# Layer 0's first attention: who subtracts the maxima of the local tiles, in how many pieces the exponential runs, and by how many rows the scores are made

## The chip, the cores and the metric

The kernel runs on one core of a Trainium2 chip. The metric is device microseconds (us) of one execution. Three executions of the kernel before took 1293.5 to 1294.74 us, with a median of 1294.52 us.

## The reference, cut to what matters

A decoder of four layers over `x` (8 batches of 128 tokens, 128 features). Each layer adds three blocks to `x`: an attention, a cross attention (or what takes its place) and a mixture of experts. The change touches only the attention of layer 0. It has 16 heads of 8 features, and each head combines three branches with a softmaxed gate: attention over compressed blocks of 16 keys, attention over the keys of the blocks chosen by rank, and attention over a local window:

```python
x = x + _L0_attn_ref(_layernorm(x, axis=-1), L0_attn_Wq, L0_attn_Wk, L0_attn_Wv, L0_attn_Wo, L0_attn_Wck, L0_attn_Wcv, L0_attn_Wg, L0_attn_bg)
```

For a head, both the chosen and the local branch start from the same scores `q @ k.T`, add their own mask (causal plus choice, or window), take the softmax over the keys of each query, and multiply by the values. A softmax does not change when the maximum is subtracted first; the kernel does so to keep the exponential in range, and divides by the sum after the values, which carry a column of ones.

## The kernel before, in words

One program holds five instruction streams (PE, VectorE, ScalarE, GpSimd and the DMA queue) that meet in semaphores. Each engine runs its stream in the order written.

The part that matters here is the loop of `layer0_attention_pe`, `_act`, `_pool` and `_dve` over 32 steps, with 9 more to drain it. Step k stands for batch k // 4 and the heads 4 * (k % 4) to 4 * (k % 4) + 3: four heads, 128 queries, 128 keys, one tile of 128x512. The work of step k:

- GpSimd multiplies the keys of the batch by a mask of four columns (`mask_keys`, L471; its line in the trace is L474), so that in each of four copies only the 8 rows of one head are left: one 128x512 tile `kM` a step. It is written up to four steps ahead, into four buffers; VectorE makes the first.
- PE multiplies all 128 rows of the queries with it (`score_pe`, L514), into banks 0 and 1 in turn.
- VectorE adds the causal mask (L874) and the window mask (L876) to the scores and so makes two tiles, chosen and local. It then takes the local tile's four maxima (`lower_dve`, L551) and multiplies them by minus the scale (L553, 128x4).
- GpSimd adds the choice of blocks to the chosen tile (L757), before the masking of keys for step k + 4.
- One step later VectorE takes the chosen tile's maxima and scales them (L551, L553 again).
- ScalarE computes `exp(scale * s + bias)` in place. The bias is a column, one for each head, so that a tile takes four instructions of 128x128 (`exp_heads_act`, L545). In a step it first copies turned tiles out of PSUM (L530), then runs the chosen tile of k - 1, then the local tile of k.
- Three steps later PE transposes both tiles (L523), ScalarE copies them out (L530), and five steps later PE multiplies the values (L534), four heads side by side.
- Once in four steps a batch is complete. ScalarE copies two banks of results (L726), PE turns them back (L540), and VectorE unpacks them in `unpack`: a reciprocal (L835), a product of 128x16 of two SBUF tiles (L837), a product with the bank (L842), and in the second unpack two sums (L858, L860). Then come a transpose (L562), its copy (L573), the output product (L567) and the sum into `x` (L578).

With k % 4 written as a residue: VectorE's unpack of the chosen heads falls ahead of the masks of a step with residue 1, the second unpack with its sums ahead of residue 2, and the sum into `x` ahead of residue 0. In PE's stream the output product opens a step of residue 0, and the scores of a step are its last work. ScalarE's copy of the results (L726) falls at residue 0, and the small copy for the output (L573) at residue 3.

The layer's cross attention (`batches_*`, from L909) already does it the other way: four copies of the keys are masked once a batch with `mask4` (L903), each of its score products takes 32 rows (L922), GpSimd subtracts the maxima (L1065), and a single exponential covers a tile (L981).

Of the kernel before, what the change touches and what calls it, by code (L numbers as in the profile page):

```python
# [11 lines left out]
ALU = mybir.AluOpType  # L12
ACT = mybir.ActivationFunctionType
AX = mybir.AxisListType

P = 128
# [104 lines left out]
def build_program(nc, d, out):  # L121
    with ExitStack() as ctx:
# [321 lines left out]
        def heads_memory(tiles, probs, outputs):  # L444
            used_ = dict(kM=[carve(4, P) for _ in range(4)], o=[carve(P) for _ in range(2)],
# [7 lines left out]
        def heads_signals(tiles, lowered=True):  # L453

            n = 4 * NB
            s = dict(km_dve=signal("km_dve", 1), km_pool=signal("km_pool", n - 1), vp=signal("vp", NB),
# [5 lines left out]
            if lowered:  # L462
                s["lowered"] = signal("lowered", n)
# [3 lines left out]

        def km_ready(eng, s, k):
            eng.wait_ge(*(s["km_pool"](k) if k else s["km_dve"](1)))

        def mask_keys(eng, kM, kT, k):  # L471

            b, g = divmod(k, 4)
            return eng.tensor_tensor(kM, kT[:, b * P:(b + 1) * P].unsqueeze(1).broadcast_to([P, 4, P]),  # L474
                                     bc(mask16[:, 4 * g:4 * g + 4], 2, P), ALU.mult)
# [14 lines left out]
        def stage_keys_pool(pool, s, m, kT, k):  # L490
            if k >= 4:
                pool.wait_ge(*s["scored"](k - 3))
            mask_keys(pool, m["kM"][k % 4], kT, k).then_inc(s["km_pool"].sem, 1)

        def stage_keys_values_pool(pool, s, m, kT, v, vp, k_out, v_out):

            pool.wait_ge(*pool_step.now())
            for k in range(2):
                pool.wait_ge(*k_out(k))
            for k in range(4 * NB):  # L500
                if k:
                    stage_keys_pool(pool, s, m, kT, k)
                if k == 1:
                    for i in range(2):
                        pool.wait_ge(*v_out(i))
                if k % 4 == 1:
                    stage_values_pool(pool, s, k // 4, v, vp, 1)

        def score_pe(pe, s, m, k, qT):
            b = k // 4  # L510
            km_ready(pe, s, k)
            if k >= 2:
                pe.wait_ge(*s["masked"](k - 1))
            pe.matmul(banks[k % 2][:, :], qT[:, b * P:(b + 1) * P], m["kM"][k % 4].rearrange("p j t -> p (j t)"),  # L514
                      start=True, stop=True).then_inc(s["scored"].sem, 1)

# [178 lines left out]
        def layer0_attention_act(act):  # L695
# [19 lines left out]
            for step in range(32 + 9):  # L715
# [21 lines left out]
                if k < 32:  # L737
# [2803 lines left out]
```

## Time and profile before

| what | value |
|---|---|
| median of three executions | 1294.52 us |
| the profiled execution: its own time | 1286.18 us |
| its span, first to last instruction | 1284.2 us |
| outside the span | 2.0 us |
| mean granted TensorE clock, share of full speed | 0.896 |
| VectorE busy in the span | 771.8 us (60%) |
| ScalarE busy | 656.8 us (51%) |
| GpSimd busy | 337.2 us (26%) |
| the loop, first to last window mask | 72.48 to 198.82 us |

How to read it: the trace times each instruction on its engine, from the span's start. A busy share over the whole span is a mean over many stages, so that what bounds this loop has to be read in its own 126 us. A timeline row gives start, duration, engine, line, operation and count, and in brackets the idle time ahead of it with the instruction that ended it. Consecutive instructions of one engine that don't depend on one another overlap by some 0.08 us.

### The profile page before, as it was taken

The numbers are of one execution on the slowest core, as the hardware profiler recorded it, in microseconds if no ns is written. First come the engines' busy times: TensorE is split into PE (matmuls) and PEld (weight loads), VectorE is DVE, ScalarE is ACT, GpSimd is POOL, SyncE is SP. The second block draws the span as 40 slices with busy tenths as digits, with TensorE's granted clock in tenths as the row PEclk, the third lists the DMA queues.
The fourth block names the chain that finished last, engine by engine and source line by source line (L and its number), as shares of the span: only waits on it lengthen the run. The fifth ranks groups of instructions, "written<-read, shape, count | busy, mean of one in ns | idle before, by whom it ended". The sixth has DMA issues, their size and how long they took to land. (4 is left out here: it accounts for less than half of the span.)

```text
span 1284.2 us, 22278 instructions
## 1 busy us (share of the span) xinstructions
PE 1010.8 (79%) x8221; PEld 758.4 (59%) x8221; DVE 771.8 (60%) x1870; ACT 656.8 (51%) x1688; POOL 337.2 (26%) x440
## 2 busy tenths in 40 slices
PE   6257877783779767779999989997789961878998
PEld 4224444352776355579976765775358850546898
DVE  4889995783323766752246665665777667764422
ACT  1168885561445646736538774775113223763433
POOL 2254542662222134410003331333410031111000
PEclk9689897896889778999999999999689995998999
DMA  7200000002555000020000000000120000000000
GB/s 246 85 1 1 2 1 18 1 1 66 150 166 198 1 1 2 2 99 1 1 2 1 2 2 1 2 2 33 79 107 26 1 1 0 2 1 1 1 1 17
DMA packets 31978, 42.46 MB, mean 33 GB/s; under 512 B 7592, under 2 KB 25632, under 8 KB 30592
## 3 DMA queue, kind: packets, MB, share of 16 engines
q1 hardware_dynamic: 30848, 38.95, 9.1%
q0 software_dynamic: 1024, 2.10, 0.5%
q8 instruction: 66, 1.08, 0.4%
q14 instruction: 40, 0.33, 0.1%
HBM read 35.54 MB, written 5.51 MB: 32 GB/s over the span
## 5 line engine op out<-in xcount | busy, mean ns | idle before, releaser
L1287 ACT ACTIVATE arena<-bank,w_L_ffn_b1T 128x512 f32<-128x512 f32 x128 | 86.9, 688 | 98.5 <-PE bank L1229 98.0
L1264 PEld LDWEIGHTS bank<-bufB,arena 128*128 128x128 f32 x1024 | 118.9, 192 | 2.4
L1264 PE MATMUL bank<-bufB,arena 128*128 128x128 f32 x1024 | 119.6, 275 | 0.0
L2525 ACT ACTIVATE arena<-arena 128x128 f32<-128x128 f32 x256 | 99.2, 390 | 20.0 <-DVE arena L2552 20.0
L293 POOL TENSOR_TENSOR norm_rstd<-norm_std,minus_half 128x4 f32<-128x4 f32 x24 | 25.4, 1060 | 316.0 <-DVE norm_std L288 316.0
L2536 POOL TENSOR_TENSOR arena<-arena 128x512 f32<-128x512 f32 x64 | 66.5, 1040 | 151.8 <-DVE arena L2585 151.8
L1324 DVE SCALAR_TENSOR_TENSOR x<-bank,gate_c,x 128x128 f32<-128x128 f32 x128 | 36.0, 344 | 114.9 <-PE bank L1264 114.7
L545 ACT ACTIVATE arena<-arena 128x128 f32<-128x128 f32 x256 | 80.3, 395 | 42.3 <-DVE arena L553 42.3
L1229 PE MATMUL bank<-x_high,w_low 128*128 128x512 f32 x200 | 85.7, 429 | 8.1 <-DVE w_low L1238 5.5
L1229 PE MATMUL bank<-x_high,w_high 128*128 128x512 f32 x200 | 81.1, 405 | 0.0
L1229 PE MATMUL bank<-x_low,w_high 128*128 128x512 f32 x200 | 81.0, 405 | 0.0
L2548 DVE SCALAR_TENSOR_TENSOR arena<-bank,bufA 128x512 f32<-128x512 f32 x64 | 43.8, 685 | 35.2 <-PE bank L2474 35.2
L2848 ACT ACTIVATE arena<-bank 128x512 f32<-128x512 f32 x36 | 21.6, 599 | 61.2 <-PE bank L1229 61.2
L514 PE MATMUL bank<-arena 128*128 128x512 f32 x64 | 37.3, 674 | 18.9 <-DVE arena L474 18.9
L2396 PE MATMUL bank<-xnT,bufA 128*128 128x512 f32 x96 | 50.7, 627 | 1.6 <-ACT arena L341 1.6
L341 ACT ACTIVATE arena<-bank 128x512 f32<-128x512 f32 x36 | 21.5, 596 | 58.7 <-PE bank L2396 39.3
L757 POOL TENSOR_TENSOR arena<-arena 128x512 f32<-128x512 f32 x32 | 33.8, 1057 | 64.4 <-DVE arena L876 64.4
L2445 PE MATMUL bank<-arena 128*64 128x128 f32 x512 | 42.1, 285 | 10.7 <-ACT arena L2516 10.5
L1229 PEld LDWEIGHTS bank<-x_high,w_low 128*128 128x128 f32 x200 | 39.4, 197 | 17.1 <-DVE w_low L1238 6.0
L2431 PEld LDWEIGHTS bank<-arena 128*128 128x128 f32 x256 | 36.7, 191 | 21.2 <-issue 14.1
L963 ACT ACTIVATE arena<-bank 128x512 f32<-128x512 f32 x64 | 36.7, 598 | 23.5 <-PE bank L939 23.1
L2525 ACT ACTIVATION_READ_ACCUMULATOR arena<-arena 128x1 f32 x256 | 48.3, 189 | 0.0
(489 smaller groups left out, 2555.6 us busy)
## 6 DMA issues: line engine op xcount, KB each, us to landing
bufB<-in_L_ffn_w SPq DMA_DIRECT2D x28, 256.0 KB
bufA<-in_L_ffn_w SPq DMA_DIRECT2D x2, 2048.0 KB, 9.8
bufB<-in_L_ffn_W SPq DMA_DIRECT2D x2, 2048.0 KB
bufB<-in_L_ffn_w SPq DMA_DIRECT2D x2, 2048.0 KB
bufA<-in_L_ffn_Wgu SPq DMA_DIRECT2D x1, 2304.0 KB, 9.0
bufA<-in_L_attn_Wqkv SPq DMA_DIRECT2D x1, 2048.0 KB, 8.8
rows<-blank SPq DMA_DIRECT2D x2, 960.0 KB, 6.9
results<-arena SPq DMA_DIRECT2D x6, 256.0 KB
```

What stands on the lines that cost most here:

```text
L514: pe.matmul(banks[k % 2][:, :], qT[:, b * P:(b + 1) * P], m["kM"][k % 4].rearrange("p j t -> p (j t)"), start=True, stop=True).then_inc(s[ ...
L545: m = act.activation(tile[:, j * P:(j + 1) * P], tile[:, j * P:(j + 1) * P], ACT.Exp, bias=low[:, j:j + 1], scale=SCALE)
L963: act.activation(m["p"][n % 4], banks[4 + n % 2][:, :], ACT.Copy).then_inc(s["probs"].sem, 1)
L1229: m = pe.matmul(bank[:, :], a[:, ws], b[:, c], start=n == 0, stop=n == 2)
L1264: i = pe.matmul(bank[:, j * P:(j + 1) * P], h[:, f, j * P:(j + 1) * P], w2[:, u * FF + f * P:u * FF + (f + 1) * P], start=f == 0, stop=f = ...
L1287: act.activation(m["h"][k % 2][:, f, :], banks[f][:, :], ACT.Gelu, bias=b1[:, c:c + 1]).then_inc(g["hidden"].sem, 1)
L2396: o = pe.matmul(bank[:, :], w[:, c * P:(c + 1) * P], xnT[:, i * BANK:(i + 1) * BANK], start=True, stop=True)
L2431: o = pe.matmul(banks[7][:, u * P:(u + 1) * P], b2["oT"][k % 2][:, j * P:(j + 1) * P], b2_wo[:, c:c + P], start=False, stop=k == UNITS - 1 ...
L2445: o = pe.matmul(banks[5 + k % 2][64 * t:64 * t + 64, j * P:(j + 1) * P], b2["v"][gg % 2][:, 4 * u + 2 * j + r, :], b2["p"][(U0 + k) % 3][: ...
L2525: o = act.activation(tile, tile, ACT.Exp, bias=b2["mn"][n % 8][:, j:j + 1], scale=-1.0, accum_out=b2["sm"][n % 8][:, j:j + 1])
L2536: pool.tensor_tensor(tile, tile, bc(b2["rs"][n % 4], 2, P), ALU.mult).then_inc(g["over_sum"].sem, 1)
L2548: dve.scalar_tensor_tensor(tile, banks[r][:, :], -1.0 / np.sqrt(DH).item(), bias[:, h0:h0 + 4, :].rearrange("p h t -> p (h t)"), ALU.mult, ...
```

## The change

Four things, in one loop:

- VectorE no longer scales the local tile's maxima; it only takes them and signals `peak`.
- GpSimd waits for `peak` and subtracts the maxima from the local tile in place (128x512), right after it has added the choice to the chosen tile.
- ScalarE computes the local tile's exponential in one instruction of 128x512, with no bias. The chosen tile keeps its four.
- The keys are masked once a batch instead of once a step: one tile `kM` of four copies, in each of which one head out of every four consecutive ones is left, in two buffers. PE's score product takes the 32 rows that hold the four heads of the step. GpSimd masks the next batch after the first subtraction of a batch. Its first use still comes from VectorE.

```diff
--- before.py
+++ after.py
@@ -442,7 +442,7 @@
 
 
         def heads_memory(tiles, probs, outputs):
-            used_ = dict(kM=[carve(4, P) for _ in range(4)], o=[carve(P) for _ in range(2)],
+            used_ = dict(kM=[carve(4, P) for _ in range(2)], o=[carve(P) for _ in range(2)],
                          oT=[carve(P) for _ in range(2)], rs=[carve(H) for _ in range(2)],
                          res=[carve(BANK) for _ in range(2)], a=[carve(BANK) for _ in range(tiles)],
                          p=[carve(BANK) for _ in range(probs)], mx=[carve(4) for _ in range(2 * 8)])
@@ -453,26 +453,17 @@
         def heads_signals(tiles, lowered=True):
 
             n = 4 * NB
-            s = dict(km_dve=signal("km_dve", 1), km_pool=signal("km_pool", n - 1), vp=signal("vp", NB),
+            s = dict(km_dve=signal("km_dve", 1), km_pool=signal("km_pool", NB - 1), vp=signal("vp", NB),
                      scored=signal("scored", n), masked=signal("masked", n), exped=signal("exped", n),
                      turned=signal("probs_turned", tiles * n), probs=signal("probs", tiles * n),
                      valued=signal("valued", tiles * n), res=signal("res", tiles * NB),
                      back=signal("heads_back", tiles * NB), weighed=signal("weighed", tiles * NB),
                      oturned=signal("o_turned", NB), oT=signal("oT", NB), projected=signal("projected", NB))
             if lowered:
-                s["lowered"] = signal("lowered", n)
+                s["peak"], s["lowered"] = signal("peak", n), signal("lowered", n)
             if tiles == 2:
                 s["chosen"], s["lowered2"], s["exped2"] = (signal(i, n) for i in ("chosen", "lowered2", "exped2"))
             return s
-
-        def km_ready(eng, s, k):
-            eng.wait_ge(*(s["km_pool"](k) if k else s["km_dve"](1)))
-
-        def mask_keys(eng, kM, kT, k):
-
-            b, g = divmod(k, 4)
-            return eng.tensor_tensor(kM, kT[:, b * P:(b + 1) * P].unsqueeze(1).broadcast_to([P, 4, P]),
-                                     bc(mask16[:, 4 * g:4 * g + 4], 2, P), ALU.mult)
 
         def pad_values_pool(pool, vp):
             for t in vp:
@@ -487,32 +478,19 @@
             pool.tensor_copy(vp[b % 4][:, :, 0:HD],
                              v[:, b * P:(b + 1) * P].rearrange("p (h c) -> p h c", c=HD)).then_inc(s["vp"].sem, 1)
 
-        def stage_keys_pool(pool, s, m, kT, k):
-            if k >= 4:
-                pool.wait_ge(*s["scored"](k - 3))
-            mask_keys(pool, m["kM"][k % 4], kT, k).then_inc(s["km_pool"].sem, 1)
-
-        def stage_keys_values_pool(pool, s, m, kT, v, vp, k_out, v_out):
-
-            pool.wait_ge(*pool_step.now())
-            for k in range(2):
-                pool.wait_ge(*k_out(k))
-            for k in range(4 * NB):
-                if k:
-                    stage_keys_pool(pool, s, m, kT, k)
-                if k == 1:
-                    for i in range(2):
-                        pool.wait_ge(*v_out(i))
-                if k % 4 == 1:
-                    stage_values_pool(pool, s, k // 4, v, vp, 1)
-
         def score_pe(pe, s, m, k, qT):
-            b = k // 4
-            km_ready(pe, s, k)
+            b, g = divmod(k, 4)
+            rows = slice(32 * g, 32 * g + 32)
+            pe.wait_ge(*(s["km_pool"](b) if b else s["km_dve"](1)))
             if k >= 2:
                 pe.wait_ge(*s["masked"](k - 1))
-            pe.matmul(banks[k % 2][:, :], qT[:, b * P:(b + 1) * P], m["kM"][k % 4].rearrange("p j t -> p (j t)"),
+            pe.matmul(banks[k % 2][:, :], qT[rows, b * P:(b + 1) * P], m["kM"][b % 2][rows, :, :].rearrange("p j t -> p (j t)"),
                       start=True, stop=True).then_inc(s["scored"].sem, 1)
+
+        def mask_batch_keys(eng, kM, kT, u):
+
+            return eng.tensor_tensor(kM, kT[:, u * P:(u + 1) * P].unsqueeze(1).broadcast_to([P, 4, P]),
+                                     bc(mask4[:, :], 2, P), ALU.mult)
 
         def turn_pe(pe, s, n, tile, exped):
 
@@ -735,8 +713,9 @@
                     exp_heads_act(act, h["a"][(2 * k) % 8], h["mx"][8 + k % 8], s["exped2"])
                 k = step
                 if k < 32:
+                    tile = h["a"][(2 * k + 1) % 8]
                     act.wait_ge(*s["lowered"](k + 1))
-                    exp_heads_act(act, h["a"][(2 * k + 1) % 8], h["mx"][k % 8], s["exped"])
+                    act.activation(tile, tile, ACT.Exp, scale=SCALE).then_inc(s["exped"].sem, 1)
 
         def layer0_attention_pool(pool):
             t, g, m, s, h = a0, a0g, a0m, a0s, a0h
@@ -747,17 +726,21 @@
             pool.wait_ge(*m.out(6))
             pool.wait_ge(*m.out(7))
             pool.wait_ge(*m.out(2))
+            pool.wait_ge(*m.out(3))
             stage_values_pool(pool, s, 0, t["v"], t["vp"], 2)
-            for k in (1, 2, 3):
-                stage_keys_pool(pool, s, h, t["kT"], k)
             for k in range(32):
                 b, gr = divmod(k, 4)
                 tile = h["a"][(2 * k) % 8].rearrange("p (r c) -> p r c", c=G0)
                 pool.wait_ge(*s["masked"](k + 1))
                 pool.tensor_tensor(tile, tile, bc(t["sel"][:, b * H + 4 * gr:b * H + 4 * gr + 4, :].rearrange(
                     "p h n -> p (h n)"), 2, G0), ALU.add).then_inc(s["chosen"].sem, 1)
-                if k + 4 < 32:
-                    stage_keys_pool(pool, s, h, t["kT"], k + 4)
+                local = h["a"][(2 * k + 1) % 8].rearrange("p (j t) -> p j t", t=P)
+                pool.wait_ge(*s["peak"](k + 1))
+                pool.tensor_tensor(local, local, bc(h["mx"][k % 8], 2, P), ALU.subtract).then_inc(s["lowered"].sem, 1)
+                if gr == 0 and b + 1 < NB:
+                    if b:
+                        pool.wait_ge(*s["scored"](4 * b))
+                    mask_batch_keys(pool, h["kM"][(b + 1) % 2], t["kT"], b + 1).then_inc(s["km_pool"].sem, 1)
                 if gr == 0 and b + 1 < NB:
                     stage_values_pool(pool, s, b + 1, t["v"], t["vp"], 2)
 
@@ -825,7 +808,7 @@
             dve.wait_ge(*dve_step.now())
             dve.tensor_scalar(t["sel"], t["sel"], 1.0, BIG, ALU.subtract, ALU.mult).then_inc(g["selected"].sem, 1)
             dve.wait_ge(*m.out(2))
-            mask_keys(dve, h["kM"][0], t["kT"], 0).then_inc(s["km_dve"].sem, 1)
+            mask_batch_keys(dve, h["kM"][0], t["kT"], 0).then_inc(s["km_dve"].sem, 1)
 
             def unpack(n, u):
 
@@ -876,7 +859,8 @@
                     dve.tensor_tensor(h["a"][(2 * k + 1) % 8].rearrange("p (j t) -> p j t", t=P), s3,
                                       bc(window[:, :], 1, 4), ALU.add).then_inc(s["masked"].sem, 1)
                     dve.wait_ge(*s["masked"](k + 1))
-                    lower_dve(dve, h["a"][(2 * k + 1) % 8], h["mx"][k % 8], s["lowered"])
+                    dve.tensor_reduce(h["mx"][k % 8], h["a"][(2 * k + 1) % 8].rearrange("p (j t) -> p j t", t=P), AX.X,
+                                      ALU.max).then_inc(s["peak"].sem, 1)
 
 
 
@@ -897,11 +881,6 @@
             else:
                 s.update(peak=signal("peak", NB), lowered=signal("lowered", 3 * NB))
             return s
-
-        def mask_batch_keys(eng, kM, kT, u):
-
-            return eng.tensor_tensor(kM, kT[:, u * P:(u + 1) * P].unsqueeze(1).broadcast_to([P, 4, P]),
-                                     bc(mask4[:, :], 2, P), ALU.mult)
 
 
         def nothing(*_):
```

## Rows read from the trace of the kernel before

**Rows 1.** Page, part 1: busy time by engine, after the span.
```profile
span 1284.2 us, 22278 instructions
```
**Rows 2.** Stretches: length, then busy time by engine, granted clock, DMA share, GB/s.
```profile
166.00:182.00 16.00, 11.75 (x115) 7.37 (x115) 15.25 (x32) 14.06 (x42) 7.97 (x9) 1.00 0.01 2
...
114.00:118.00 4.00, 4.00 (x22) 2.48 (x14) 2.28 (x6) 4.00 (x13) 1.93 (x2) 0.57 0.00 0
```
**Rows 3.** Waits in 70 to 210 us: who for whom, us in total, times, longest.
```profile
DVE arena L874 <- PE bank L514: 7.3, 8, 2.2
```
**Rows 4.** Timeline, window mask of steps 23 to 27, 30 and 31.
```profile
166.44 0.67 DVE L876 TENSOR_TENSOR arena<-bank,window 128x512 f32<-128x512 f32 x1
...
170.04 0.68 DVE L876 TENSOR_TENSOR arena<-bank,window 128x512 f32<-128x512 f32 x1
...
174.53 0.68 DVE L876 TENSOR_TENSOR arena<-bank,window 128x512 f32<-128x512 f32 x1
...
179.67 0.68 DVE L876 TENSOR_TENSOR arena<-bank,window 128x512 f32<-128x512 f32 x1
...
183.02 0.68 DVE L876 TENSOR_TENSOR arena<-bank,window 128x512 f32<-128x512 f32 x1
...
195.56 0.68 DVE L876 TENSOR_TENSOR arena<-bank,window 128x512 f32<-128x512 f32 x1
...
198.82 0.68 DVE L876 TENSOR_TENSOR arena<-bank,window 128x512 f32<-128x512 f32 x1
```
**Rows 5.** Timeline, step 26 to step 27, a step without an unpack.
```profile
180.43 1.05 POOL L757 TENSOR_TENSOR arena<-arena 128x512 f32<-128x512 f32 x1 [3.08 <-DVE arena L876]
181.10 0.40 DVE L553 TENSOR_SCALAR arena<-arena 128x4 f32<-128x4 f32 x1
181.44 1.04 POOL L474 TENSOR_TENSOR arena<-arena,mask 128x512 f32<-128x512 f32 x1
181.51 0.69 DVE L551 TENSOR_REDUCE arena<-arena 128x4 f32<-128x512 f32 x1
181.54 1.28 ACT L545 ACTIVATE arena<-arena 128x128 f32<-128x128 f32 x4 [1.08 <-DVE arena L553]
182.24 0.27 DVE L553 TENSOR_SCALAR arena<-arena 128x4 f32<-128x4 f32 x1
```
**Rows 6.** Timeline, from step 26's exponentials to the scores of step 28.
```profile
182.72 0.25 ACT L573 ACTIVATE arena<-bank 128x128 f32<-128x128 f32 x1
...
183.03 0.49 PE L567 MATMUL bank<-w_L_attn_Wo,arena 128*128 128x128 f32 x2 [1.83 <-ACT arena L573]
...
184.96 1.02 PE L514 MATMUL bank<-arena 128*128 128x512 f32 x2
...
186.02 0.69 DVE L874 TENSOR_TENSOR arena<-bank,causal 128x512 f32<-128x512 f32 x1 [0.17 <-PE bank L514]
```
**Rows 7.** Timeline, step 23's exponentials (with step 22's), and the wait of step 29.
```profile
167.26 2.44 ACT L545 ACTIVATE arena<-arena 128x128 f32<-128x128 f32 x8
...
190.45 0.69 DVE L874 TENSOR_TENSOR arena<-bank,causal 128x512 f32<-128x512 f32 x1 [0.48 <-PE bank L514]
```
**Rows 8.** Timeline, the small product of the unpack, beside a GpSimd instruction and alone.
```profile
176.56 0.81 DVE L837 TENSOR_TENSOR arena<-arena 128x16 f32<-128x16 f32 x1
...
188.66 0.18 DVE L837 TENSOR_TENSOR arena<-arena 128x16 f32<-128x16 f32 x1
```
**Rows 9.** Groups by line, 0 to 300 us: count, busy us, mean ns, idle before.
```profile
L1065 POOL TENSOR_TENSOR arena<-arena,bufB 128x512 f32<-128x512 f32 x32 | 33.2, 1040 | 17.9 <-DVE bufB L1039 17.5
...
L981 ACT ACTIVATE arena<-arena 128x512 f32<-128x512 f32 x32 | 20.1, 629 | 18.4 <-POOL arena L1065 18.4
...
L858 DVE TENSOR_TENSOR arena<-arena 128x128 f32<-128x128 f32 x8 | 2.3, 292 | 0.3
```
**Rows 10.** Timeline, four score products of the cross attention, 32 rows each.
```profile
242.51 1.14 PE L922 MATMUL bank<-bufB 32*128 32x512 f32 x8
```
**Rows 11.** Timeline, the two longest waits for scores inside the loop, steps 12 and 16.
```profile
117.61 0.69 DVE L874 TENSOR_TENSOR arena<-bank,causal 128x512 f32<-128x512 f32 x1 [1.65 <-PE bank L514]
...
136.06 0.69 DVE L874 TENSOR_TENSOR arena<-bank,causal 128x512 f32<-128x512 f32 x1 [1.67 <-PE bank L514]
```

## The prediction

> **What bounds it now.** The profiled execution took 1286.18 us, 2.0 more than its span [rows 1], and is 8.3 us below the median of the runs shown, 1294.52. I work a difference out in the profiled one and put it on the median. I take 0.2%, 2.6 us, as what a measurement of this kernel can tell from no change.
>
> The first view is the stretches. In 166 to 182 us VectorE is busy for 15.25 of 16 us, ScalarE for 14.06, PE for 11.75, GpSimd for 7.97, at the full clock [rows 2]. So VectorE looks like the bound, and ScalarE is near. The waits say that PE isn't far either: VectorE waits for its scores in eight steps, 7.3 us in all [rows 3].
>
> The timeline gives the rhythm. I write t for the start of a step's window mask (L876). The period at the full clock is 3.60, 4.49, 5.14 and 3.35 us: 16.58 from step 23 to 27 [rows 4]. I call a step by its k % 4.
>
> A plain step shows what VectorE is busy with [rows 5]. GpSimd adds the choice from t + 0.76 to t + 1.81. VectorE's scaling of four columns starts at t + 1.43, and takes 0.40 us: it ends 0.02 us after GpSimd's instruction. The second scaling takes 0.27 and ends 0.03 after the masking of keys. The product L837 is clearer: 0.81 us beside a masking of keys, 0.18 without one [rows 8]. So part of VectorE's "busy" is waiting for GpSimd to let go. The maxima of the chosen tile start at 181.51, 0.03 after GpSimd's 181.48: they wait for the chosen tile, not for the scaling.
>
> **The parts of the change.**
>
> *The scaling that goes.* 32 instructions of 0.40, some 13 us of VectorE's busy time. In a plain step nothing of it comes back: the next instruction waits for GpSimd's addition until t + 1.84 anyway [rows 5], and the other scaling stays held until t + 2.84, now by the subtraction in the masking's place. Residues 3 to 0 and 2 to 3 keep their length on VectorE's side. In a step with an unpack the reciprocal can start at t + 1.32 instead of t + 1.76. L837 then asks for the port at t + 1.60, during the addition, gets it as the scaling did, and ends at t + 1.84 instead of t + 2.84: 1.0 us earlier.
>
> *The subtraction on GpSimd.* 32 of 1.04 us [rows 9], for the 31 maskings of 1.04 that shrink to 7. GpSimd goes from 8.0 to about 9 of 16 us: not a bound. But the subtraction holds the port from t + 1.77 to t + 2.81. Of the second unpack, L842 reads a bank and passes; L858 (two SBUF tiles as L837, 0.29 alone) follows at t + 2.19, is held, and ends near 2.96 rather than 2.48 [rows 9]. So the interval of residue 1 to 2 gets 1.0 - 0.48, say 0.54, shorter: 4.60 for 5.14. No row shows L858 beside a GpSimd instruction; its ends are no hold (1.0 gained) and a full hold (0.5), and I take the hold, since L837 has the same form. The Trainium skill (SBUF — State Buffer, "Who interferes with whom") says the same of forms: two SBUF inputs contend with a GpSimd instruction that reads SBUF, a reduction or an instruction with one SBUF input doesn't, and the loser is blocked for the whole instruction. By it the gain is 0.5 and not 1.0.
>
> In the first unpack L842 is followed by the maxima and the kept scaling, which asks at t + 2.79, when the subtraction ends and the batch's masking (1.04) follows. If it loses the port it ends at t + 3.86; if it wins, at t + 2.98. I take the loss, an interval of 4.38; the win would be 3.5. At the full clock this decides nothing (below); in the two periods whose residue 0 comes late by a low clock [rows 11] the scores are ready by then, and a win is worth 0.8 each.
>
> *The signal to ScalarE comes later.* `lowered` was ready at t + 1.84, and will be at t + 2.85, after the addition and the subtraction. The exponential then takes 0.63 us instead of 1.28 [rows 5, 9]. It ends at t + 3.51, not t + 3.15: **0.36 later**. What waits for it is PE. In rows 6, step 26's exponential lets the small copy start at 182.72, the output product, values, transposes and scores of step 28 follow in PE's order, and the scores end at 185.98; VectorE, free at 185.85, waits 0.17. So from t(26) to t(28) the chain takes 6.96 us and sets the time. With 0.36 more it is 7.32, and the interval of residue 3 to 0 grows from 3.60 to 3.97.
>
> The same holds for the next one. Step 23's exponentials end at 169.70 = t + 3.26 [rows 7]; the copy of the results, the turn back, the values, transposes and scores of step 25 follow, and its mask starts at t(23) + 7.48. With the exponential ending at 3.51 that is 0.25 more, against 0.05 of slack: t(25) comes at t(23) + 8.29, not 8.09. That these scores are near the bound is shown in step 29: there L837 takes 0.18, and VectorE waits 0.48 for PE instead [rows 7, 8]. VectorE's own side, 3.97 + 4.38 = 8.35, is about the same. The 1.0 us gained in the first unpack is hence lost to the scores.
>
> *ScalarE.* 96 fewer instructions: 2.56 us of exponentials a step become 1.9. It is relieved, but it waits at every exponential, so that only the 0.65 counted above matters.
>
> *PE.* A product of 32 rows, two passes. Four of them took 1.14 us together [rows 10], one of 128 rows 1.02 [rows 6]. Apart from the first two, the new ones stand alone between transposes. I take 1.02 as before; the ends are 0.28 (the share of four) and 1.14. At the low end each score would come 0.74 us sooner, which would undo the 0.36 and give back up to 0.4 more a score-bound interval (some ten of them, -7 us with the 0.36s): I give it little, since each of the four is one of eight passes issued back to back.
>
> *Keys once a batch.* Each masking is ready three steps ahead, so the scores never wait. At the start the second score no longer waits for GpSimd's, but the first addition began at step 0's mask both ways: nothing. The added wait for the second half of the keys was over before the loop. No DMA is moved.
>
> **The sum.** A full-clock period: +0.26 for residues 3 to 1, -0.54, 0: -0.3. Five such periods have a masking of keys beside the unpack; where the period starts without the output product (once) or after a late step (once) the gain is 0.2: about -1.2 in all. The interval from step 3 to 4, at PE's pace, +0.36. The last period had no masking of keys to hold VectorE. Step 28's window mask is at 186.63, 0.61 after row 186.02 [rows 6]. From there to step 30 it took 8.93 and will take 4.32 + 4.60, and to step 31 it goes from 3.26 to 3.35 [rows 4]; with the 0.36 in front, +0.4. The drain starts from an exponential 0.2 later: +0.2. Total: -0.2 us, or -2 with the port won at residue 1. **Forecast: no change; in the profiled execution 1286.0 us, on the median 1294.3.**
>
> **The rivals.**
>
> *A, 50%: the sum holds*, from -2.5 to +2: 1292 to 1296.5.
>
> *B, faster, 27%.* The waits for scores are longest where the clock is low: 0.57 in 114 to 118 us [rows 2]; there VectorE waits 1.65 us for its scores, and 1.67 in step 16 [rows 11], each time 1.5 us more than the 0.17 of step 28. If a shorter second unpack, which shortens PE's pause in it, keeps the clock up, 3 us come back; if L858 isn't held, 0.5 in five periods; if the port is won, 1.6. Two of them, the first among them, give -4.6 to -5.5: about 1289.5. Against: the pauses that precede the low stretches are those of the output product.
>
> *C, slower, 23%.* That pause grows: PE has nothing from the end of step 27's scores to the output product, 1.83 us before [rows 6] and some 2.3 after. A long wait followed it in two of six periods. If it follows in all, four more at 1.5 are +6 us: 1300. It decides from two more on (+2.8). A lesser form of it: L837 just misses the port, which brings back 0.54 in five periods, +2.4.
>
> That the exponential of 128x512 isn't quicker than four is excluded by rows 9, where it takes 0.63.
>
> The range, 1289.5 to 1299, reaches to B and most of the way to C's 1300; what it leaves out is C in full and short scores. Chances: faster 0.27, same 0.50, slower 0.23.
>
> **What would show it.** The exponential's row 0.63 us, starting near t + 2.88. The chosen maxima in plain steps still at t + 1.84. L837 near 0.25 us; L858 near 0.75 in the second unpack; residue 1 to 2 at 4.6. VectorE's wait for scores (7.3 us) above 10, GpSimd's subtraction 1.04. The loop from 72.5 to some 198.5. Wrong would be: scores on time at residue 0, L837 still 0.8, or a change of the low-clock stretches.

## The result, and the profile of the changed kernel

The changed kernel takes 1304.0 us in the median of 13 runs, against 1294.5 for the kernel before: a ratio of 1.0088, with an interval from 1.0067 to 1.0110. It is slower by some 11 us. The forecast was no change, 1294.3 us, and its range ended at 1299.

The two profiled executions differ by more, 1302.2 against 1284.2 us of span, because the one of before was a short one (1286.18 us, where the median is 1294.5). The last sum into `x` of this attention starts at 227.0 us and not at 217.8. That is 9.2 us, about the difference of the medians (9.5), and the part that the change can explain. I look no further for the rest. The two rows, before and changed:

```profile
217.83 0.29 DVE L578 TENSOR_TENSOR x<-x,bank 128x128 f32<-128x128 f32 x1 [1.73 <-PE bank L567]
```

```profile
226.96 0.29 DVE L556 TENSOR_TENSOR x<-x,bank 128x128 f32<-128x128 f32 x1 [1.73 <-PE bank L545]
```

Page, part 1, of the changed kernel:

```profile
span 1302.2 us, 22159 instructions
```

The stretch 72 to 212 us, which holds the loop in both, first of the kernel before, then of the changed one (length; busy time of PE, PE's loads, VectorE, ScalarE, GpSimd; granted clock):

```profile
72.00:212.00 140.00, 102.63 (x908) 63.08 (x906) 121.94 (x255) 117.67 (x343) 64.24 (x68) 0.91 0.00 1
```

```profile
72.00:212.00 140.00, 115.64 (x809) 66.30 (x808) 109.14 (x213) 90.38 (x231) 73.82 (x78) 0.78 0.00 1
```

VectorE and ScalarE have less to do, as meant: 109 and 90 us of 140 instead of 122 and 118. Part of that is only that the changed kernel gets less far in the stretch; over the whole execution, where both kernels do the same work, VectorE is busy for 763.0 us instead of 771.8 and ScalarE for 636.7 instead of 656.8. PE is busy for longer, though the stretch ends before the changed kernel's drain, and its granted clock fell from 0.91 to 0.78. The waits of the changed kernel between 70 and 215 us say where that goes:

```profile
DVE arena L857 <- PE bank L487: 21.1, 13, 2.7
```

VectorE waited for scores for 7.3 us in eight steps [rows 3]; now it is 21.1 us in thirteen. L857 is the causal mask (L874 before), and L487 the score product (L514 before).

Summed over the loop's 31 intervals between window masks, by the residue of the step (step number modulo 4):

| from residue to residue | before, us | changed, us |
|---|---|---|
| 0 to 1 | 33.7 | 36.6 |
| 1 to 2 | 37.3 | 34.3 |
| 2 to 3 | 27.1 | 28.3 |
| 3 to 0 | 28.2 | 37.8 |
| all | 126.3 | 137.1 |

The loop is 10.8 us longer and the drain behind it 1.9 us shorter. Two of the 10.8 us are lost at once: the intervals from step 3 to 5, ahead of any output product, take 9.56 us for 7.47. In both kernels the clock is low when the loop starts; the kernel before has the full clock from some 73.5 us on (but for 83.7 to 87.1), the changed one only from some 91 us on. The stretch 76 to 82 us, before and changed:

```profile
76.00:82.00 6.00, 1.87 (x10) 0.81 (x8) 5.77 (x12) 4.20 (x15) 4.11 (x4) 1.00 0.00 0
```

```profile
76.00:82.00 6.00, 4.23 (x10) 1.93 (x10) 4.98 (x9) 3.20 (x10) 4.65 (x6) 0.50 0.00 0
```

One period of the changed kernel, from its timeline. L859 is the window mask (L876 before), L735 and L739 are GpSimd's addition and subtraction, L529 and L531 VectorE's maxima and scaling of the chosen tile, L718 the single exponential, L545 the output product and L501 the transposes:

```profile
113.49 1.10 PE L501 MATMUL bank<-ident,arena 128*128 128x128 f32 x8
...
114.52 1.12 PE L487 MATMUL bank<-arena 32*128 32x512 f32 x2
...
114.68 1.06 POOL L735 TENSOR_TENSOR arena<-arena 128x512 f32<-128x512 f32 x1 [2.55 <-DVE arena L859]
115.70 1.04 POOL L739 TENSOR_TENSOR arena<-arena 128x512 f32<-128x512 f32 x1
115.77 0.69 DVE L529 TENSOR_REDUCE arena<-arena 128x4 f32<-128x512 f32 x1 [0.45 <-POOL arena L735]
116.49 0.27 DVE L531 TENSOR_SCALAR arena<-arena 128x4 f32<-128x4 f32 x1
...
116.77 0.63 ACT L718 ACTIVATE arena<-arena 128x512 f32<-128x512 f32 x1 [1.85 <-POOL arena L739]
117.28 0.68 DVE L859 TENSOR_TENSOR arena<-bank,window 128x512 f32<-128x512 f32 x1
...
117.62 0.49 PE L545 MATMUL bank<-w_L_attn_Wo,arena 128*128 128x128 f32 x2 [1.98 <-ACT arena L551]
...
118.94 1.97 PE L501 MATMUL bank<-ident,arena 128*128 128x128 f32 x8
...
120.84 1.49 PE L487 MATMUL bank<-arena 32*128 32x512 f32 x2
...
122.37 0.69 DVE L857 TENSOR_TENSOR arena<-bank,causal 128x512 f32<-128x512 f32 x1 [2.25 <-PE bank L487]
...
122.97 0.68 DVE L859 TENSOR_TENSOR arena<-bank,window 128x512 f32<-128x512 f32 x1
```

With t = 113.92 for the window mask of that step, the chosen maxima start at t + 1.85, and the exponential at t + 2.85 for 0.63 us. These answer to 1.84 and 1.28 us in [rows 5], and to the prediction's t + 1.84 and t + 2.88. Then the transposes, which take 1.10 us at the full clock, take 1.97, and the interval is 5.69 us instead of 3.60 [rows 4]. PE's clock in those microseconds, from the view by stretches:

```profile
117.00:118.00 1.00, 0.38 (x2) 0.30 (x2) 0.97 (x3) 1.00 (x4) 0.00 (x0) 1.00 0.00 0
118.00:119.00 1.00, 1.00 (x18) 0.58 (x17) 0.87 (x2) 1.00 (x4) 0.97 (x1) 0.60 0.00 0
119.00:120.00 1.00, 1.00 (x6) 1.00 (x6) 0.84 (x2) 0.70 (x3) 1.00 (x2) 0.50 0.00 0
...
121.00:122.00 1.00, 1.00 (x2) 0.34 (x2) 0.00 (x0) 1.00 (x3) 0.00 (x0) 0.69 0.00 0
```

From some 118.2 to 121.6 us the clock is at the lower of its two levels (0.50, that is 1.2 GHz for 2.4). Five intervals from residue 3 to 0 hold an output product (the sixth product falls into the drain). In the kernel before two of them ran low, at 5.10 us; here all five do. In three of the five the clock falls at the output product, as above. In the other two, the steps 16 and 24, it had fallen some 4 us earlier, behind a pause of 1.41 us ahead of the transpose L540 (L562 before):

```profile
130.67 0.33 PE L540 MATMUL bank<-ident,arena 128*128 128x128 f32 x1 [1.41 <-DVE arena L843]
...
132.00:133.00 1.00, 1.00 (x6) 0.78 (x4) 0.96 (x3) 0.94 (x4) 0.31 (x1) 0.50 0.00 0
...
135.63 0.80 PE L545 MATMUL bank<-w_L_attn_Wo,arena 128*128 128x128 f32 x2 [0.45 <-ACT arena L551]
```

Where the clock is full, the changed kernel's intervals are 3.36, 4.36 and 4.60 us, no longer than the prediction had them. But for some 0.2 us in one step (3.57 us), what the loop loses it loses where the clock is low.

Three of VectorE's lines in the changed kernel (min, median and max in ns): the small product of the unpack (L837 before), the first sum of the second unpack (L858 before) and the kept scaling (L553 before):

```profile
L820 DVE TENSOR_TENSOR arena<-arena x16: 174/248/704, 104.8 to 224.1; 128x16 f32<-128x16 f32 x16
...
L841 DVE TENSOR_TENSOR arena<-arena x8: 291/754/757, 111.5 to 224.6; 128x128 f32<-128x128 f32 x8
...
L531 DVE TENSOR_SCALAR arena<-arena x32: 169/268/1039, 75.3 to 212.4; 128x4 f32<-128x4 f32 x32
```

### The profile page after: what moved, and what is told of

Read it like the earlier page. It is cut to its first block and busy times, and to the rows that moved or that the text cites. A ratio compares the mean times of both kernels' runs of the same rounds, so it can differ in the third digit from the quotient of the medians.

```text
span 1302.2 us, 22159 instructions
## 1 busy us (share of the span) xinstructions
PE 1037.1 (80%) x8221; PEld 774.8 (59%) x8221; DVE 763.0 (59%) x1838; ACT 636.7 (49%) x1592; POOL 345.5 (27%) x448
## 5 line engine op out<-in xcount | busy, mean ns | idle before, releaser
L2504 ACT ACTIVATE arena<-arena 128x128 f32<-128x128 f32 x256 | 99.2, 390 | 19.9 <-DVE arena L2531 19.9
L487 PE MATMUL bank<-arena 32*128 32x512 f32 x64 | 43.7, 800 | 20.4 <-DVE arena L492 18.9
L718 ACT ACTIVATE arena<-arena 128x512 f32<-128x512 f32 x32 | 20.2, 630 | 72.7 <-POOL arena L739 72.7
L501 PE MATMUL bank<-ident,arena 128*128 128x128 f32 x256 | 47.3, 343 | 6.9 <-ACT arena L508 6.1
L735 POOL TENSOR_TENSOR arena<-arena 128x512 f32<-128x512 f32 x32 | 33.9, 1058 | 68.0 <-DVE arena L859 68.0
L2424 PE MATMUL bank<-arena 128*64 128x128 f32 x512 | 42.1, 285 | 10.8 <-ACT arena L2495 10.5
```

The lines of the kernel that those rows point to most:

```text
L487: pe.matmul(banks[k % 2][:, :], qT[rows, b * P:(b + 1) * P], m["kM"][b % 2][rows, :, :].rearrange("p j t -> p (j t)"), start=True, stop=Tr ...
L501: t = pe.transpose(banks[2 + n % 2][:, j * P:(j + 1) * P], tile[:, j * P:(j + 1) * P], ident[:, :])
L2424: o = pe.matmul(banks[5 + k % 2][64 * t:64 * t + 64, j * P:(j + 1) * P], b2["v"][gg % 2][:, 4 * u + 2 * j + r, :], b2["p"][(U0 + k) % 3][: ...
L2504: o = act.activation(tile, tile, ACT.Exp, bias=b2["mn"][n % 8][:, j:j + 1], scale=-1.0, accum_out=b2["sm"][n % 8][:, j:j + 1])
```

## Two theories and the first four experiments

Two things in the change could do it. Theory **P**, my rival C: the later exponential makes PE's pause ahead of the output product longer, and the clock falls after it. Theory **R**: score products that use 32 of PE's 128 rows cost clock, and they are slower in themselves. I had not thought of R. Each half of the change was tried alone, R's edit alone, and all but R's edit. In this section the kernel before had a median of 1278.9 us on the chip used, and every ratio is to it.

**Scores by 32 rows, alone.** The kernel before, with one edit. The rows left out of the masked keys are zeros, so the result is the same:

```diff
-            pe.matmul(banks[k % 2][:, :], qT[:, b * P:(b + 1) * P], m["kM"][k % 4].rearrange("p j t -> p (j t)"),
+            rows = slice(32 * (k % 4), 32 * (k % 4) + 32)
+            pe.matmul(banks[k % 2][:, :], qT[rows, b * P:(b + 1) * P], m["kM"][k % 4][rows, :, :].rearrange("p j t -> p (j t)"),
```

> The kernel before, with one edit: the score product takes the 32 rows that are not zero instead of all 128; masking of keys, lowering and exponentials stay. Theory R (rows): the low clock comes with the products of 32 rows, and each also takes 0.2 us longer; then this alone is 5 to 10 us slower than before, the attention ends at 222 to 227 us instead of 217.8, and the clock falls after the output product in every period. Theory P (pause): the clock falls because PE's pause ahead of the output product ends later and is longer when the exponential comes 0.36 us later; then this stays within 0 to 3 us of before and the clock stays as before.

Measured: 1296.2 us, a ratio of 1.0128 (1.0083 to 1.0173). The attention ends at 236.7 us instead of 217.8. Its stretch 72 to 212 us, and rows of its timeline (L515 is its score product, L568 the output product, L524 the transposes, L875 and L877 the masks):

```profile
72.00:212.00 140.00, 121.21 (x760) 68.69 (x759) 112.38 (x229) 103.72 (x305) 63.62 (x68) 0.71 0.00 1
```

```profile
141.47 0.49 PE L568 MATMUL bank<-w_L_attn_Wo,arena 128*128 128x128 f32 x2
...
146.35 0.66 PE L541 MATMUL bank<-ident,arena 128*128 128x128 f32 x4 [1.74 <-ACT arena L727]
...
147.80 1.97 PE L524 MATMUL bank<-ident,arena 128*128 128x128 f32 x8
149.69 2.07 PE L515 MATMUL bank<-arena 32*128 32x512 f32 x2
151.81 0.69 DVE L875 TENSOR_TENSOR arena<-bank,causal 128x512 f32<-128x512 f32 x1 [2.31 <-PE bank L515]
152.41 0.68 DVE L877 TENSOR_TENSOR arena<-bank,window 128x512 f32<-128x512 f32 x1
...
155.65 2.07 PE L515 MATMUL bank<-arena 32*128 32x512 f32 x2
...
158.37 0.68 DVE L877 TENSOR_TENSOR arena<-bank,window 128x512 f32<-128x512 f32 x1
```

The clock is 0.71, lower than in the changed kernel, with lowering, exponentials and maskings as before. And the low stretch does not sit where P puts it: the output product at 141.47 follows the scores with no pause ahead of it (its row has no bracket), and the clock is down six microseconds later, over two whole steps (147.8 to 158 us; an interval of 5.96). A pause does come just before that fall, but another one: 1.74 us ahead of the turn back (L541), which the kernel before has too, up to 1.76 us long, with no fall behind it inside the loop. R is borne out, with 17 us where I gave it 5 to 10. The clock of the whole execution says so in every run: 0.870 to 0.875 in all six, 0.891 to 0.903 in 28 of the 29 of the kernel before (0.860 in one). My expectation had placed the fall after every output product; that part was wrong, since here the scores are so late that the output product no longer waits.

**The keys' part alone**, 32 rows included: the changed kernel with VectorE's scaling and ScalarE's four pieces put back.

```diff
-                pool.wait_ge(*s["peak"](k + 1))
-                pool.tensor_tensor(local, local, bc(h["mx"][k % 8], 2, P), ALU.subtract).then_inc(s["lowered"].sem, 1)
...
-                    act.activation(tile, tile, ACT.Exp, scale=SCALE).then_inc(s["exped"].sem, 1)
+                    exp_heads_act(act, h["a"][(2 * k + 1) % 8], h["mx"][k % 8], s["exped"])
```

> The changed kernel with VectorE scaling the local maxima and ScalarE in four pieces again, so that only the keys once a batch and the scores by 32 rows are left of the change. Theory R: 3 to 8 us slower than before (GpSimd's missing maskings give back up to 0.6 us a period). Theory P: no slower, likely 2 to 4 us faster, since the unpack is no longer held by a masking and the exponential is as early as before.

Measured: 1290.3 us, 1.0092 (1.0055 to 1.0130); clock 0.73 in 72 to 212 us. P wanted it faster than before. It is as slow as the whole change, and slower than I gave R: 11 us and not 3 to 8.

**The lowering alone**, with keys once a step and 128 rows, so that GpSimd has three instructions a step:

```diff
+                pool.wait_ge(*s["peak"](k + 1))
+                pool.tensor_tensor(local, local, bc(h["mx"][k % 8], 2, P), ALU.subtract).then_inc(s["lowered"].sem, 1)
...
-                    exp_heads_act(act, h["a"][(2 * k + 1) % 8], h["mx"][k % 8], s["exped"])
+                    act.activation(tile, tile, ACT.Exp, scale=SCALE).then_inc(s["exped"].sem, 1)
```

> The kernel before with only the other half of the change: GpSimd subtracts the local maxima and one exponential covers the tile; keys masked once a step, scores by 128 rows. GpSimd now has three instructions a step. Theory R: within -2 to +4 us of before, L514 at 1.02 us at the full clock, low-clock stretches about as before. Theory P: 6 to 10 us slower, a low clock after each output product.

Measured: 1282.8 us, 1.0021 (0.9991 to 1.0051); clock 0.87. The interval holds 1. The chain's 0.36 us and a somewhat lower clock are there: its intervals from residue 3 to 0 with an output product are 5.0 to 5.6 us in four of five, and its loop takes 131.5 us for 126.3 in that one profiled execution. So P is not nothing, but it isn't the 9 us: its interval ends at 0.5%, some 6.5 us, and that of the whole change begins at 0.67%. The clock of the whole execution, 0.893 to 0.904 in its twelve runs, is that of the kernel before.

```profile
72.00:212.00 140.00, 103.58 (x842) 62.91 (x841) 113.76 (x217) 94.57 (x240) 96.95 (x101) 0.87 0.00 1
```

**All of the change but the rows.** GpSimd also masks the queries once a batch, into four copies that keep 32 rows each; a product takes one such copy and the whole key tile.

```diff
-            pe.matmul(banks[k % 2][:, :], qT[rows, b * P:(b + 1) * P], m["kM"][b % 2][rows, :, :].rearrange("p j t -> p (j t)"),
+            pe.matmul(banks[k % 2][:, :], m["qM"][b % 2][:, g, :], m["kM"][b % 2].rearrange("p j t -> p (j t)"),
...
+                    mask_batch_queries(pool, h["qM"][(b + 1) % 2], t["qT"], b + 1)
```

> The changed kernel with scores by 128 rows: GpSimd also masks the queries once a batch, four copies of which each keeps 32 rows, and the product takes such a copy and the four-column keys whole. Same results, one GpSimd instruction of 1.04 us more a batch. Theory R: 5 to 9 us faster than the changed kernel, that is within 2 to 4 us of before, score products of 1.02 us and few low-clock stretches. Theory P: as slow as the changed kernel, a low clock after each output product.

Measured: 1280.5 us, 1.0020 (0.9997 to 1.0043); clock 0.92, as before. The products that count are the same as with 32 rows, and the other 96 rows of the stationary side hold zeros; the clock comes back all the same. So it is the rows used, not what is in them. The ratio to before is 0.7 points lower than the changed kernel's, some 9 us; the two were measured on different chips, each beside the kernel before, and their intervals lie apart. Three of its five intervals from residue 3 to 0 are still low (5.49 to 5.56 us). In the others my sum can be read at the full clock. One of them (L867, L869: the masks; L489: the scores; L552: the output product), under its stretch:

```profile
72.00:212.00 140.00, 100.77 (x874) 62.59 (x872) 112.01 (x222) 95.44 (x243) 81.26 (x85) 0.92 0.00 1
...
153.10 0.67 DVE L869 TENSOR_TENSOR arena<-bank,window 128x512 f32<-128x512 f32 x1
...
153.44 0.49 PE L552 MATMUL bank<-w_L_attn_Wo,arena 128*128 128x128 f32 x2 [2.17 <-ACT arena L558]
...
155.37 1.02 PE L489 MATMUL bank<-arena 128*128 128x512 f32 x2
...
156.43 0.69 DVE L867 TENSOR_TENSOR arena<-bank,causal 128x512 f32<-128x512 f32 x1 [0.50 <-PE bank L489]
157.04 0.68 DVE L869 TENSOR_TENSOR arena<-bank,window 128x512 f32<-128x512 f32 x1
```

From residue 3 to 0 it takes 3.94 us, for the 3.97 of the prediction; the other intervals of a period are 4.35, 4.60 and 3.35, for 4.38, 4.60 and 3.35. PE's pause ahead of the output product is longest here, 2.17 us, and still the stretch has the clock of before.

The start of the loop sorts all the kernels run. In 76 to 82 us, ahead of any output product, the granted clock is 0.50 in all five whose scores use part of the rows (the changed one, the two above that keep it, and the two of the next section that do) and 1.00 in all seven whose scores use all 128. No output product comes before that stretch, and so no pause of P.

## What part of the rows costs, and the pause

**The pause filled.** The changed kernel with eight transposes ahead of each output product, into bank 6, which nobody reads then:

```diff
+                        if k == step - 9:
+                            for j in range(8):
+                                pe.transpose(banks[6][:, (j % 4) * P:(j % 4 + 1) * P], ident[:, :], ident[:, :])
```

> The changed kernel with eight transposes of the identity (128 rows, 1.1 us at the full clock) added ahead of each output product, into a bank that nobody reads then: they fill about half of PE's pause of 1.98 us and delay nothing at the full clock. Theory R, as the first four runs bear it out: full-array work ahead of the fall helps, since the products of 32 rows leave PE just under what the clock wants; the time comes 2 to 8 us below the changed kernel. Theory P in its weak form (the pause triggers it): the low stretch after the output product disappears, 6 to 10 us below. If neither pause nor rows at this place matter: within 2 us of the changed kernel.

Measured: 1300.7 us beside 1292.3 for before on that chip, 1.0082 (1.0051 to 1.0114), where the changed kernel had 1.0088. Three of its five intervals with an output product are 5.64, 5.36 and 5.64 us; the other two are 3.9, but each is followed by one of 6.07 where 4.35 is usual, so there the fall came one step later. Filling a good half of the pause (0.96 us of it are left) bought nothing in the total, so that pause alone isn't what lets the clock fall; what full work would suffice, and where, this doesn't say. My expectation for R failed here too: work in all rows ahead of the fall was to help by 2 to 8 us.

**64 rows.** The kernel before with the half that holds the step's heads:

```diff
+            rows = slice(64 * (k % 4 // 2), 64 * (k % 4 // 2) + 64)
```

> The kernel before with the score product by 64 rows, the half that holds the four heads; everything else as before. It asks whether the cost comes with any product of part of the rows or grows as the rows shrink. If it grows with the rows left out: between before and the 32-row kernel, 4 to 10 us slower than before. If 64 rows already count as the whole: within 2 us. If any part costs all of it: 12 to 17 us, as with 32 rows. A pass of 64 rows lasts 0.59 us if it is like the whole, 0.69 if it is like 32 rows.

Measured: 1288.0 us, 1.0090 (1.0057 to 1.0123), beside 1278.9 for before. It lies between the whole and 32 rows (1.0128), if only just: the intervals of the two overlap, and 9 us is at the upper end of what I gave a graded cost. The clock of the whole execution is 0.869 to 0.886 in its nine runs, beside 0.892 to 0.902 in the twenty of the kernel before on that chip. Its stretch:

```profile
72.00:212.00 140.00, 117.59 (x801) 67.49 (x803) 118.32 (x242) 108.83 (x320) 63.80 (x68) 0.78 0.00 1
```

The length of a pass is not graded. A score product runs in two passes. Line by line (min, median and max of a pass in ns), first the 32-row products of the changed kernel, then the 64-row ones, then the 128-row ones of the fastest kernel below:

```profile
L487 PE MATMUL bank<-arena x64: 587/692/1218, 70.0 to 207.6; 32*128 32x512 f32 x64
```

```profile
L515 PE MATMUL bank<-arena x64: 589/693/1219, 70.4 to 209.7; 64*128 64x512 f32 x64
```

```profile
L489 PE MATMUL bank<-arena x64: 592/595/1219, 71.5 to 191.3; 128*128 128x512 f32 x64
```

The medians, 0.69 and 0.595 us, mix the two passes of a product, and some at the low clock. Taken singly, the two of the changed kernel's product at 114.52 are

```profile
114.52 0.69 PE L487 MATMUL bank<-arena 32*128 32x512 f32 x1
...
115.05 0.59 PE L487 MATMUL bank<-arena 32*128 32x512 f32 x1
```

So it is the first pass that grows, from 0.595 to 0.69 us; the second takes 0.59 either way, and the product 1.12 for 1.02. In the rows of the period above, transposes and scores run from 113.49 to 115.64, 2.15 us; before, the same two took 1.95 (184.03 to 185.98). So a partial product costs PE 0.2 us at the full clock. It stays hidden there: the intervals at the full clock are no longer than with all rows. What is paid is the clock's fall.

## A version that beats both

Two kernels take the good half of the change. With keys and queries masked once a batch, 128-row scores, and the lowering of before, no masking holds VectorE's unpack. A second edit takes the output product out of the scores' way:

```diff
-                for k in (step - 9, step - 8):
-                    if k % 4 == 3 and 0 <= k < 32:
-                        output_pe(pe, s, h, k // 4, W["L0_attn_Wo"][:, :], turn=k == step - 8)
+                k = step - 8
+                if k % 4 == 3 and 0 <= k < 32:
+                    output_pe(pe, s, h, k // 4, W["L0_attn_Wo"][:, :], turn=True)
...
                     score_pe(pe, s, h, step, t["qT"])
+                k = step - 9
+                if k % 4 == 3 and 0 <= k < 32:
+                    output_pe(pe, s, h, k // 4, W["L0_attn_Wo"][:, :], turn=False)
```

with `add_dve` moved to the end of VectorE's step in the same way. First each alone, then both.

> The kernel before with the output product (and VectorE's sum into x) moved from the front of its step to behind the scores. It tests what my sum called the chain of residue 3 to 0: the scores no longer wait for the output's copy. If that chain bounds the interval: 3.35 to 3.45 us instead of 3.60 at the full clock, and 4.0 to 4.6 instead of 5.1 at the low one; in all 1 to 5 us faster. If it doesn't: no change.

Measured, the output product behind, on the kernel before: 1291.8 against 1292.3 us, 0.9991 (0.9974 to 1.0008). The intervals from residue 3 to 0 are 3.36 us at the full clock and 4.3 to 4.7 at the low one, for 3.60 and 5.10 before, about as expected. But three of five were low in its profiled execution instead of two, and of the 1 to 5 us that I expected no difference is left in the total.

> Keys and queries masked once a batch, scores by 128 rows, and the lowering and the four exponentials of before: the part of the change that frees the port, without 32-row products and without the late exponential. By the last period of the trace of before (4.43, 4.50, 3.26 us) a period takes 15.8 to 15.9 instead of 16.58 us: 4 to 5 us faster than before, if the clock stays as in before. If the clock falls more often, within 2 us of it.

Measured: 1289.9 us, 0.9985 (0.9963 to 1.0007). Its period is 4.59, 4.50, 3.26 and 3.70 us, 16.05 at the full clock; two of five still ran low after the output product. The 0.5 us a period is there in the trace; of the 4 to 5 us that I expected, the medians show 2.4, and the total can't be told from no change.

> The two before it together. If both hold, the period goes to 15.5 us or less and the whole is 5 to 9 us faster than before; if the output product only moves the wait to another step, as the one without it.

Measured: 1288.2 us, 0.9968 (0.9948 to 0.9988), 4 us where I expected 5 to 9. A second time:

> The version with keys and queries masked once a batch, 128-row scores and the output product behind them, a second time and with more rounds, beside the 64-row kernel on one chip. If its gain of 0.3% is real: a ratio to before of 0.995 to 0.998, interval below 1, and from step 16 on periods near 15.9 us with the clock full.

Measured: 1272.4 beside 1278.9 us, 0.9956 (0.9937 to 0.9974). From step 11 on each period takes 3.30, 4.83, 4.51 and 3.26 us, 15.9 together, and the clock stays full up to the drain. Its stretch 72 to 212 us:

```profile
72.00:212.00 140.00, 99.19 (x922) 61.34 (x922) 121.12 (x268) 116.96 (x344) 49.51 (x53) 0.96 0.00 1
```

The clock is 0.96, the highest of all these kernels, and PE is busy for the fewest microseconds. This version is 4 to 6 us faster than the kernel before and, by the ratios, some 16 us faster than the change.

## Why the prediction was wrong

- **The step that failed** is the one on PE: "I take 1.02 as before; the ends are 0.28 (the share of four) and 1.14." The product takes 1.12, near the upper end, and starts 0.1 us later behind the transposes, so 0.2 us where I had nothing. But what mattered wasn't on the list at all: no term for what the shape does to the clock. The upper end had no clock in it. One edit of rows alone costs 1.28%. The forecast left the low-clock stretches as they were, and the rivals tied them to PE's pauses alone; "a change of the low-clock stretches", one of its signs of being wrong, is what came: clock 0.78 for 0.91, and 10.8 us in the loop.
- **The chain.** That a later exponential delays the scores by 0.36 us, and that residue 3 to 0 goes from 3.60 to 3.97, was right: 3.94 where the clock is full. VectorE is near its bound, but each period's length is set where it waits for PE, and there the lower clock is paid in full: 5.6 to 6.2 us five times, instead of 5.1 twice.
- **The port.** Right in each of its times. L837, now L820, has a median of 0.25 us for the 0.81 of [rows 8]. L858, now L841, has one of 0.754 us for 0.292 [rows 9]: it is held by the subtraction, as the Trainium skill (SBUF — State Buffer, "Who interferes with whom") says of two SBUF inputs beside a GpSimd instruction that reads SBUF. The kept scaling lost the port to the batch's masking: its longest, 1.04 us, start when the subtraction ends. That scaling has one SBUF input, so the prediction's "a reduction or an instruction with one SBUF input doesn't" says too much: that section of the Trainium skill makes an exception of VectorE's 2-port modes, which a scaling (`tensor_scalar`) can enter. Residue 1 to 2 takes 4.60 us, to the hundredth. The loop's 37.3 us there fell to 34.3.
- **Rival C** had the sign, much of the place and about the size (1300, from more low stretches after the output product), with 23%. Its mechanism was not the main one. The pause grew from 1.83 [rows 6] to 1.98 us only, not to 2.3; half filled, it changed nothing in the total. With 128 rows it grew to 2.17, close to C's figure, and there the late exponential costs 0.2%, which the measurement can't tell from nothing.
- **C's own reading** was off in two points. The loop holds five output products; the sixth falls into the drain, where the clock fell behind it in the kernel before too. So "all" is three more at 1.5 us, 4.5 and not 6. And "the pauses that precede the low stretches are those of the output product" holds for only one of its two steps, 12. Ahead of step 16 the clock of the kernel before was low already when the output product came; it fell behind a pause of 2.02 us ahead of the transpose L562:

```profile
126.58 0.33 PE L562 MATMUL bank<-ident,arena 128*128 128x128 f32 x1 [2.02 <-DVE arena L860]
...
128.00:129.00 1.00, 1.00 (x6) 0.94 (x5) 0.97 (x3) 0.64 (x3) 0.04 (x1) 0.54 0.02 8
...
131.57 0.79 PE L567 MATMUL bank<-w_L_attn_Wo,arena 128*128 128x128 f32 x2 [1.05 <-ACT arena L573]
```

- **The sum's own size** was right for what it covered: all of the change but the rows measured 1.0020 with an interval that holds 1, beside a forecast of no change.

What stays open is why fewer rows lower the granted clock although they raise PE's busy time, and how many of the low stretches the later exponential adds: the totals leave it anything from nothing to 0.5%. The runs show the dependence (128, 64, 32 rows: clock 0.91, 0.78, 0.71 in this stretch, from one profiled execution each), not its rule.

## What to carry to other kernels

The zero rows of a matmul operand cost nothing here: cutting the product to the rows that count made the product longer and the clock lower, while masking the queries as well, so that all 128 rows stay in use, kept both. Before an edit of a PE instruction's shape is costed by its duration, look how often the clock is already low in that stage; where it sometimes is, the shape may decide it. And when work moves to GpSimd, look for VectorE's instructions with two SBUF inputs, or small scalings, that will fall beside it: they end when GpSimd's does.

## What the runs showed of the hardware that was not expected

- Fewer rows, lower clock: 0.91 with 128 rows, 0.78 with 64, 0.71 with 32, in 72 to 212 us of otherwise equal kernels. Zeros in the full-row product do no harm (0.92). It needs more than 32-row products as such, though: this kernel's cross attention issues four of them back to back, 1.14 us in all [rows 10], and has the full clock, 1.00, in every four microseconds from 244 to 280 in the kernel before.
- Of the two passes of a lone product by 32 or 64 rows the first takes 0.69 us, for 0.595 with 128 rows; the second takes 0.59 in all.
- Less work for VectorE and ScalarE (9 and 20 us over the execution) bought nothing in the changed kernel.
